# Two graph layers in one kernel: the target nodes' message projection made in layer two, four pairs of tiles ahead of its use, in place of layer one's dense steps

## The reference

```python
# layer one: attention-weighted sum of neighbours, per head
feat = relu(einsum('nd,ohdk->ohnk', feat_in, W) + b)
edge_w = (att_s[:, row] + att_n[:, col]) * adj_vals
agg = segment_sum(edge_w[..., None] * feat[1][:, col, :], row)
x = _layernorm(x + normalized(concat(feat[0], agg)))
# layer two: a message per edge, summed at one end
msg_in = concatenate([x[row], x[col]], axis=-1)         # row = src, col = dst
messages = relu(msg_in @ W_msg + b_msg)
aggregated = segment_sum(messages, col)
h = relu(concatenate([x, aggregated], axis=-1) @ W_upd + b_upd)
x = _layernorm(x + _layernorm_with_gamma_beta(h))
```

## Time and profile before

| | us |
|---|---|
| median of 3 executions | 4562.25 |
| lowest and highest | 4553.59, 4563.39 |
| the profiled execution's own time | 4582.59 |
| its span in the profile | 4580.9 |

### The profile page before, as it was taken

The page is one execution under the profiler, slowest core; times in us unless marked ns, Lnnn a source line. Parts: engine busy times, 40 slices in busy tenths (PEclk is TensorE's granted clock), DMA queues, the critical chain, the costliest instruction groups (busy, mean ns, idle before and its releaser), DMA issues.

```text
span 4580.9 us, 86838 instructions
## 1 busy us (share of the span) xinstructions
PE 3871.1 (85%) x26503; PEld 3220.8 (70%) x26503; DVE 3467.5 (76%) x7782; ACT 2778.8 (61%) x7161; POOL 2709.3 (59%) x2816
## 2 busy tenths in 40 slices
PE   3999999899999999994878777778777777877876
PEld 2999999788888888883656666656566665656655
DVE  7999999799999999983666666666666666666665
ACT  3777777777667767762555555555555555555554
POOL 2887999543333343334666666666666666666662
PEclk9999999999999999997888988989888988989988
DMA  4676444566666666653455455555555545445544
GB/s 126 222 229 215 180 172 171 189 189 191 196 190 189 192 195 191 189 171 117 146 145 151 150 149 149 150 152 147 150 147 152 148 145 151 147 145 152 151 145 85
DMA packets 377690, 752.23 MB, mean 164 GB/s; under 512 B 60164, under 2 KB 205015, under 8 KB 377203
## 3 DMA queue, kind: packets, MB, share of 16 engines
q0 software_dynamic: 115680, 361.28, 29.0%
q1 hardware_dynamic: 261554, 385.37, 24.9%
HBM read 551.87 MB, written 196.16 MB: 163 GB/s over the span
## 4 chain that ended last, share of the span: by engine, by line
PE 54%; issue 16%; DVE 16%; another core or an unknown queue 8%; DVEq 2%; SPq 1%; DMA 1%; ACT 1%; POOL 1%; ACTq 0%; POOLq 0%
PE ps L1244 19%; PE ps L1266 11%; PE ps L1277 10%; DVE big L1798 6%; PE ps L1226 4%; DVE arena L1808 3%; PE ps L1086 2%; PE ps L1297 2%; PE ps L1299 2%; PE ps L1097 1%; DVE big L1517 1%; DVEq L1798 1%; PE ps L1081 1%; DVE big L1526 1%
## 5 line engine op out<-in xcount | busy, mean ns | idle before, releaser
L761 POOL DMA_INDIRECT arena<-d_p,tabs x1628 | 1559.5, 958 | 904.2 <-issue 466.9
L1266 PE MATMUL ps<-arena 128*128 128x256 f32 x3256 | 930.9, 426 | 274.6 <-DVE big L1798 206.3
L1808 DVE TENSOR_TENSOR arena<-arena,ps 128x512 f32<-128x512 f32 x814 | 532.6, 684 | 767.6 <-remote 441.4
L1277 PE MATMUL ps<-big,scr 128*128 x3256 | 858.0, 404 | 278.9 <-DVE arena L1808 203.7
L1054 ACT ACTIVATE arena<-arena 128x1024 f32<-128x1024 f32 x407 | 430.1, 1057 | 1071.6 <-DVE arena L1808 911.8
L1266 PEld LDWEIGHTS ps<-arena 128*128 128x128 f32 x3256 | 648.6, 209 | 488.9 <-ACT arena L1054 228.9
L1277 PEld LDWEIGHTS ps<-big,scr 128*128 128x128 f32 x3256 | 652.0, 204 | 420.9 <-issue 322.0
L747 POOL DMA_INDIRECT arena<-d_m,scr x392 | 462.9, 1181 | 718.7 <-DVE arena L1653 386.3
L1798 DVE SCALAR_TENSOR_TENSOR big<-big,tabs,ps 128x256 f32 x1628 | 775.6, 476 | 109.3 <-DVE big L1798 51.9
L1244 PE MATMUL ps<-arena,scr 128*128 128x256 f32 x2620 | 611.2, 383 | 2.0 <-DVE arena L1653 2.0
L943 ACT ACTIVATE arena<-arena 128x128 f32<-128x128 f32 x1310 | 410.7, 389 | 218.8 <-PE ps L1244 207.8
(11 more groups left out here) (281 smaller groups left out, 6018.2 us busy)
## 6 DMA issues: line engine op xcount, KB each, us to landing
arena<-d_loc SPq DMA_DIRECT2D x407, 256.0 KB
d_m<-arena SPq DMA_DIRECT2D x108, 603.0 KB
d_m<-arena SPq DMA_DIRECT2D x108, 402.0 KB
arena<-d_p,tabs POOLq DMA_INDIRECT x1628
arena<-in_xT_dram SPq DMA_DIRECT2D x96, 256.0 KB
d_xp<-arena SPq DMA_DIRECT2D x49, 256.0 KB, 2.8
arena<-d_xp SPq DMA_DIRECT2D x49, 256.0 KB
d_x<-arena SPq DMA_DIRECT2D x49, 256.0 KB
```

The costliest lines, as they stand in the source:

```text
L761: e.indirect_dma_start(out=G1[j % 8][:, k, :], out_offset=None, in_=d_p, in_offset=bass.IndirectOffsetOnAxis(ap=tabS[:, j, k:k + 1], axis= ...
L1266: m = e.matmul(turn(H, AB)[:, k * 256:k * 256 + 256], OH1[(j - 2) % 4][:, 2 * h + k, :], G1[(j - 2) % 8][:, 2 * h + k, :], start=True, sto ...
L1277: m = e.matmul(turn(H, QB)[:, k * 256:k * 256 + 256], OT1[j % 2][:, 2 * h + k, :], big[:, ts[2 * h + k] + 1, :], start=True, stop=True)
L1808: e.tensor_tensor(v, v, q2(turn(2 * j + h, QB)[:, :]), ALU.add).then_inc(S("f_m"), 1)
```

## The change

Pairs 0 to 3 (`QL = 4`) keep step 17 and 18 in layer one. For the 45 pairs from 4 on, Q is made in layer two: at steps o = 5 and o = 6 of `node1(p, o)` TensorE makes Q of pair p+4 in the empty bank `PG`, one tile in each step, from two new buffers `XTQ`, and at o = 7 ScalarE copies it to `big`. SyncE loads the two buffers from `d_y` (two loads of 128 KB) at o = 0, after the earlier use of the buffers is over (`g_qm`). TensorE waits for the copies (`g_qc`) ahead of the queries of an iteration that may need them and ahead of a pair's step 0, which writes `PG` again. The half of `W_msg` that makes Q must stay in `wm`, so the lower half of `W_upd` is loaded over the other half (`WUB`). A flag for edge lists in which Q would be needed too early is worked out with four small VectorE operations in the preparation, and joined to the flag that was there.

```diff
+QL = 4
+SPAN = 11
+def pq(p, n):
+    return p + min(p, QL) + n
+def ahead(j):
+    return max(0, min(NP, int((4 * j + 3 + SPAN) / 16.5) // 2 + 1) - QL)
...
+        XTQ = [take(2, 128)]
...
+        XTQ.append(scr[:, 4608:4864].rearrange("p (a b) -> p a b", a=2))
...
-        WUB = WU[:, 2:4, :]
+        WUB = wm[:, :, 0:256]
...
                     if o == 0:
                         waitn(e, "g_mm", p - 1)
                         e.dma_start(XTL[p % 2].rearrange("p a b -> p (a b)"), d_y[p * 128:(p + 1) * 128, :]).then_inc(S(f"g_in{p % 2}"), 16)
+                        if p + QL < NP:
+                            waitn(e, "g_qm", p)
+                            for b in range(2):
+                                e.dma_start(XTQ[b].rearrange("p a b -> p (a b)"), d_y[(p + QL) * 128:(p + QL + 1) * 128, b * 256:(b + 1) * 256])\
+                                 .then_inc(S("g_xq"), 16)
...
-                if o == 18:
-                    waitn(e, "b_mm", 2 * p + 2)
+                if o == 18 and p < QL:
+                    waitn(e, "b_mm", pq(p, 1) + 1)
                     e.activation(big[:, 2 * p + 1:2 * p + 3, :], q2(PS[3][:, :]), ACT.Copy).then_inc(S("b_pq"), 1)
...
                 if o == 7:
                     waitn(e, "g_v1", p + 1)
                     e.activation(sm(p, 100, 2), sm(p, 98, 2), ACT.Sqrt).then_inc(S("g_sq"), 1)
+                    q = p + QL
+                    if q < NP:
+                        waitn(e, "g_qm", p + 1)
+                        e.activation(big[:, 2 * q + 1:2 * q + 3, :], q2(PG[:, :]), ACT.Copy).then_inc(S("g_qc"), 1)
...
-                if o in (15, 17):
+                if o == 15 or (o == 17 and p < QL):
                     n = (o - 15) // 2
                     waitn(e, "b_xt", p + 1)
-                    waitn(e, "b_pq", 2 * p + n)
+                    waitn(e, "b_pq", pq(p, n))
...
                     waitn(e, "f_ot", j + 1)
+                    waitn(e, "g_qc", ahead(j))
...
                 if o == 0:
                     waitn(e, "g_re", p)
+                    waitn(e, "g_qc", min(p, NP - QL))
...
+                if o in (5, 6) and p + QL < NP:
+                    b = o - 5
+                    waitn(e, "g_re", p + 1)
+                    waitn(e, "g_xq", 32 * (p + 1))
+                    for k in range(2):
+                        m = e.matmul(PG[:, b * 256:(b + 1) * 256], XTQ[b][:, k, :], wm[:, k, 256:512], start=(k == 0), stop=(k == 1))
+                    if b == 1:
+                        m.then_inc(S("g_qm"), 1)
...
+            A1(e.tensor_scalar(fsl[:, 0:NT], c[:, C_IO:C_IO + NT], 16.5, -float(SPAN), ALU.mult, ALU.add))
+            A1(e.tensor_tensor(fsl[:, 0:NT], fsl[:, 0:NT], a[:, 0:NT], ALU.subtract))
+            A1(e.tensor_reduce(ovs, fsl[:, 0:NT], AX.X, ALU.max))
+            A1(e.scalar_tensor_tensor(ovF, ovs, 0.0, ovF, ALU.is_gt, ALU.add))
```

More of the change, by code:

```diff
@@ L59 @@
 A_CHUNK = A_TILE + 4
-A_BIAS = A_CHUNK + 9 + 2 * 5 + 1
+A_BIAS = A_CHUNK + 13 + 2 * 5 + 1
 A_LOC = A_BIAS + 1
@@ L96 @@
 SHARED.update({"ump": ("u0p", 2 * 1600), "u1p": ("s_val", NB + NGA), "ufp": ("ip", 3), "umv": ("tb", T_DONE), "u_w": ("u_l", 96)})
+SHARED.update({"g_qm": ("s_tr", 4 * NB), "g_qc": ("s_sel", 4 * NB), "g_xq": ("tab", 16 * 8)})
 def wait(e, sem, v):
@@ L642, in _ @@
                     if o == 17:
-                        waitn(e, "b_pq", 2 * p + 1)
+                        waitn(e, "b_pq", pq(p, 0) + 1)
                         e.dma_start(pair(d_p, p), PB).then_inc(S("b_s3"), 16)
@@ L649, in _ @@
             waitn(e, "b_x", NP)
-            waitn(e, "b_mm", 2 * NP)
+            waitn(e, "b_mm", pq(NP, 0))
             e.dma_start(WUB, Wu[256:512, :].rearrange("(k p) n -> p k n", p=128)).then_inc(s_w, 16)
@@ L985, in node @@
                 if o == 14:
-                    waitn(e, "b_mm", 2 * p)
+                    waitn(e, "b_mm", pq(p, 0))
                     waitn(e, "b_s4", 16 * p)
@@ L991, in node @@
                     waitn(e, "b_s3", 16 * p)
-                    waitn(e, "b_mm", 2 * p + 1)
+                    waitn(e, "b_mm", pq(p, 0) + 1)
                     e.activation(PB, q2(PS[3][:, :]), ACT.Copy).then_inc(S("b_pq"), 1)
-                if o == 18:
-                    waitn(e, "b_mm", 2 * p + 2)
+                if o == 18 and p < QL:
+                    waitn(e, "b_mm", pq(p, 1) + 1)
                     e.activation(big[:, 2 * p + 1:2 * p + 3, :], q2(PS[3][:, :]), ACT.Copy).then_inc(S("b_pq"), 1)
@@ L1211, in node @@
                 if o == 13:
-                    waitn(e, "b_pq", 2 * p)
+                    waitn(e, "b_pq", pq(p, 0))
                     waitn(e, "b_xt", p)
@@ L1252, in _ @@
                     node(p, o)
-            waitn(e, "b_pq", 2 * NP)
+            waitn(e, "b_pq", pq(NP, 0))
             e.wait_ge(s_At, len(TABS + FIRSTS))
```

## The result

| | before | after |
|---|---|---|
| median, us | 4557.92 (4 runs, 4548.22 to 4563.39) | 4486.78 (4 runs, 4483.40 to 4490.03) |
| profiled execution, its span, us | 4582.59, 4580.9 | 4490.03, 4488.4 |
| first gather of layer two, us from the span's start | 2091.5 | 2022.1 |
| from there to the span's end, us | 2489.4 | 2466.3 |

The ratio is 0.9846, with an interval of 0.9834 to 0.9858: the change takes 71.1 us off (65 to 76), where the forecast took 47. The profiled execution of before lies 25 us above this median, that of after 3 us. So of the last line's 23 us, some 21 are the profiled execution's own, and what the change did lies in the line above it: 69.4 us, all of it ahead of layer two.

A forecast was written before the change was run, and what follows sets the result against it. It took TensorE to bound layer one and no engine to be full in layer two. Layer one -61, ScalarE and tail -2, layer two +15, preparation +1 gave -47 us: 4515 us from a median of 4562.25, range 4474 to 4553.

The forecast's parts named there:

- A: The forecast itself: layer one gives 50 to 71 us, layer two takes back 0 to 35; 4490 to 4535; chance 0.55.
- B: Layer one: VectorE takes TensorE's place as limit, gain 34 us in place of 61; 4542 to 4552; chance 0.13.
- TensorE sets layer one: Layer one: TensorE is busy for 1000 of 1000 us, so step 17's 1.73 us counts in full for 42 pairs.
- The two floors: Layer one: VectorE's floor 22.38 us a round and TensorE's 22.33 are equal, and coupled engines don't both reach it.
- The friction of the forecast: Layer one: 1.45 us gained a round in place of 1.73, times 42 gives 61 us, ends 34 and 71.
- The +1: Preparation: four more small operations of about 0.26 us, started 0.3 us apart, cost 1 us.
- The -2 for ScalarE and the tail: End of layer one: 2 us gained from ScalarE's dropped copy and the shorter dependency of pairs 46 and 47.
- I take 15: Layer two: the 77.8 us of moved matmuls cost 15 us on the path, ends 0 and 77.8.
- C: Layer two: the moved matmuls keep TensorE's clock up and save about 41 us; 4474; chance 0.15.
- D: Layer two is TensorE's after all, so the moved matmuls cost their time; 4578 to 4604; chance 0.09.
- E: Layer two: the new SyncE wait or 11.8 MB more DMA lengthens unexplained waits by 44 us; 4559; chance 0.08.
- What it said would show: Signs: layer one's round about 22.6 us, VectorE 97%, TensorE some 98%; layer two within 35 us, TensorE busy 80 to 90 more.

The follow-up runs named there:

- e9_bias_in_q: Changed kernel with the message bias put on Q in layer two in place of P in layer one; 4120.55 us, 0.9788 of the kernel before.
- e2_both: Changed kernel with Q of pairs 4 to 48 made in layer one again as well as in layer two; 4211.65 us, 0.9999 of the kernel before.
- e3_mm_only: Kernel before plus two unused matmuls at each of steps 5 and 6 of 45 pairs, without loads or copies; 4213.63 us, ratio 1.0000.
- e1_copy_only: Changed kernel without the loads and matmuls of Q in layer two, ScalarE's copies kept; 4141.76 us, 0.9832 of the kernel before.
- e7: Kernel before plus 8 unused matmuls at each of steps 5 and 6 of 45 pairs; 4213.92 us, ratio 1.0008.
- e12_before3: Kernel before with three gathers in place of four per layer-two iteration from the ninth on; 4046.75 us against 4592.39, ratio 0.8823.
- e5_after: The changed kernel, unchanged, run on the second chip; 4133.69 us, 0.9818 of the kernel before.
- e10_3gathers: Changed kernel with three gathers in place of four per layer-two iteration from the ninth on; 3814.15 us, 0.9060 of the kernel before.

## Why the prediction was right, and where its sizes were off

The direction and the mechanism held: 4486.78 us lies in the range of 4474 to 4553, 28 us below the number. It lies 3 us below A's own range, 4490 to 4535: the gain is 71 us and not 47, as both of A's larger terms, layer one's and layer two's, came out at their favourable ends. Two ends don't follow from the prediction's own terms: -50 - 2 + 35 + 1 gives A 4546 and not 4535, and B with layer two at its chain share (-34 - 2 + 36 + 1) gives 4563 and not 4552.

**TensorE sets layer one: right.** The whole 1.73 us came off each of the 42 rounds, 72.5 us in all.

**"The two floors are then 22.38 and 22.33 us: equal. Two engines at the same floor ... don't both reach it": mis-sized.** TensorE's floor was exact, VectorE's is 22.08. The 22.3 us of small gaps in 1000 us were right, 0.54 a round before and in e9_bias_in_q. The error is in "907.78 busy": 21.84 a round before, 430.80 / 20 = 21.54 in e9_bias_in_q, for the same operations of the same length (L1650 took 131.0 us for 160, as L1691 does). The timelines of VectorE show where most of the 0.3 us goes, before and then e9_bias_in_q:

```profile
1669.45 0.82 DVE L1650 TENSOR_TENSOR scr<-scr,arena 128x640 f32<-128x640 f32 x1 [0.68 <-issue]
1671.06 0.82 DVE L1653 TENSOR_TENSOR arena<-arena 128x640 f32<-128x640 f32 x1 [0.78 <-ACT arena L943]
1671.80 0.20 DVE L1693 RECIPROCAL small<-ps 128x8 f32<-128x8 f32 x1
```
```profile
1506.27 0.81 DVE L1691 TENSOR_TENSOR scr<-scr,arena 128x640 f32<-128x640 f32 x1
1507.01 0.82 DVE L1694 TENSOR_TENSOR arena<-arena 128x640 f32<-128x640 f32 x1
1507.74 0.42 DVE L1729 TENSOR_REDUCE ps<-arena 128x8 f32<-128x256 f32 x1
```

Where another operation is queued behind it, one of these operations is followed after 0.74 us (1506.27 to 1507.01), though its record is 0.82 long; the records overlap by 0.08. Ahead of a wait (here the 0.78 us ahead of 1671.06) they don't, and the 0.08 counts as busy. The round of before that begins at 1667.20 us has three such waits, 0.24 of the 0.30 us, and they go when the waits go. So VectorE had 1.98 us a round to shed, more than TensorE's 1.73, and was never the limit. The friction of the forecast (1.45 in place of 1.73) rested on an equality that wasn't there: 42 x 1.73 = 72.7 us is what this term should have said in place of 61, and 72.5 is what it measured. B's "gain 34" needed that L1650's waits don't shrink; they fell from 27.4 us to 1.8.

**ScalarE, the tail, the preparation.** The +1 is about right: the first group of messages began 1.3 us later, pair 0's P 1.9. The -2 for ScalarE and the tail had the wrong sign: from P of pair 46 to the first gather it took 1.3 us longer.

**"I take 15" for layer two: mis-sized, its lower end was right.** e2_both and e3_mm_only give 0 within 4 us, and e1_copy_only agrees. The reason that the prediction gave for a small number, a floor of GpSimd's behind it, is what sets layer two on these chips: 1.27 us a gather, 5.08 an iteration. On the chip of the first pair an iteration takes 5.9 us and GpSimd waits now and then. That the cost is about 0 there too follows from the medians, 71.1 us less of which 69.4 lie ahead of layer two, with the interval's 5 us of doubt and the few us by which the start of layer two differs between runs; it wasn't tested by itself on such a chip. There it can also be a cost and a gain through the clock that cancel.

**C, the clock.** It did rise: on the first pair's chip from 0.89 to 0.92 over layer two, on the others from 0.97 to 0.98 with the change and to 1.00 with 8 matmuls. The Trainium skill has it so in "TensorE: Matmul & The Clock Gate", section on the HAM clock gate (activity releases the gate). The trace agrees with the rule. On the chips of e3 and e7 the time didn't move with it: TensorE wasn't what layer two waited for. On the first pair's chip the 41 us that C expected aren't there, since the medians leave 2 us for layer two; whether a smaller gain hides there, no run shows.

**D and E.** D fell by e2_both; the point at which TensorE decides is between 8 and 16 matmuls a step. Two of the signs that the prediction named for them did show on the first pair's chip, 34 us more of GpSimd's waits behind the sums and 60 us more of unexplained ones ahead of the messages, and layer two wasn't longer: such waits are no cost by themselves where others shrink by as much. SyncE's new waits (E) are small in after, over layer two (total, times, longest):

```profile
SPq L677 <- DVE scr L1821: 1187.3, 168, 34.7
...
SPq L691 <- remote: 38.2, 6, 8.6
SPq L691 <- PE ps L1335: 3.9, 3, 1.5
```

**What it said would show.** VectorE at 97% and vanishing waits: right (869.05 of 900 is 96.6%). TensorE at 98% with waits for L1653: wrong, it stayed at 100%; that, 22.33 us and not 22.6, is where the 11 us of the first term were. Layer two within 35 us: right. TensorE's busy time there grew by 67 us and not by 80 to 90 (1851.32 to 1918.21 for the same 1598 gathers), while its idle time shrank by 87 (529 to 442): at the higher clock its other matmuls took less, L1266's records 426 ns on the mean and L1292's 416.

## What to carry to other kernels

Work moved from a stretch that one engine fills to one where another engine sets the pace earns its full duration, if the room there is larger than the work; adding dummy work of growing size at the new place measures that room in a few runs (here 8.6 us a pair for 1.73). Before counting a second engine's busy time as its floor, subtract what its waits add: here each wait kept two records from overlapping, and VectorE's busy time fell from 21.84 to 21.54 us a round when the waits went. Then try what else can leave the full engine on the same terms: the bias alone gave 13.7 us more, down to VectorE's floor.

## What the runs showed that was not expected

**Two kinds of chips.** The kernel before takes 4558 us on the first pair's chip and 4592 on that of e12_before3, but 4211 to 4215 on three others. With so few chips, whether the chip or the moment makes the difference isn't shown. It is in layer two alone: that begins at 2091.5 and at 2093.4 us, and lasts 2489 or 2115. On the first kind VectorE's messages wait 400 to 500 us for something that the trace doesn't show (L1848 above), on the other for the gathers. Groups of e5_after, 2150 to 4000 us:

```profile
L783 POOL DMA_INDIRECT arena<-d_p,tabs x1459 | 1406.2, 964 | 444.6 <-issue 436.0 <-PE ps L1292 8.5
...
L1848 DVE TENSOR_TENSOR arena<-arena,ps 128x512 f32<-128x512 f32 x730 | 470.6, 683 | 361.4 <-DMA arena<-d_p,tabs 321.1 <-PE ps L1304 36.6
```

The chip that has these waits also shows one of 25 us at the start of layer two, in both kernels; in the chain of after:

```profile
2034.53 1.57 issue
2037.19 25.52 another core or an unknown queue
```

GpSimd issues gathers every 1.25 us all through it, and from 2045 to 2062 us TensorE, ScalarE and VectorE stand still. The message that waits needs a count of TensorE's queries and the landing of a gather; which of the two came late, the trace doesn't say. In e12_before3, with three gathers an iteration, the same waits are 84.3 us for 582 messages (2150 to 3500 us), where before has 256.1 for 455: they shrink with the gathers. What makes them stays open. It bears on the reading of the earlier trace rows: the 16.2% and 439.7 us there belong to the chip and not to the kernel.

**Gathers have a price by the piece.** 128 rows of 1 KB take GpSimd 0.95 us and 0.3 us until the next, with four or three an iteration; what part of the 0.95 goes into descriptors, the trace doesn't say. The Trainium skill, "DMA: Bandwidth & Descriptors", section "Anatomy of one DMA — SWDGE (gpsimd) path", calls descriptor generation small and says that many can be emitted before the cost shows. By that alone one wouldn't look to GpSimd's issuing for what sets layer two; e5_after's chain and e10_3gathers show that it is there, and the measurement decides.
